# Two mixture-of-experts stages of a perceiver kernel: the order of norms, logits and first-layer products, who splits the weights, and the order of the output products

## The reference, cut to what matters

```python
xn = layernorm(x)                                    # (2048, 128), no gain or bias
logits = xn @ Wr + br                                # (2048, 8)
# mixture 1: probs = softmax(logits); comb = probs where in the token's top 2, else 0
y1 = sum(comb[:, e] * (gelu(xn @ W1[e] + b1[e]) @ W2[e] + b2[e]) for e in range(8))    # hidden 192
# mixture 2: comb = softmax over the top 2 logits alone
y2 = sum(comb[:, e] * ((silu(xn @ W1[e] + b1[e]) * (xn @ W2[e] + b2[e])) @ W3[e] + b3[e])
         for e in range(8))                                                            # hidden 512
x = x + y
```

## Time and profile before

| what | value |
| --- | --- |
| median of three runs | 3657.43 us (3654.14 to 3657.65) |
| the profiled execution, its own time | 3659.62 us |
| its span in the trace | 3656.9 us |
| PE busy over the span | 3368.5 us (92%) |
| DVE, ACT, POOL busy | 2508.6, 1895.5, 1145.4 us |
| mixture 1, from its first transfer to the last copy on ACT | 1280.6 to 1427.7 us |
| mixture 2, from its first transfer to the last addition on DVE | 3264.1 to 3650.3 us |

### The profile page before, as it was taken

The page is one execution under the profiler, slowest core; times in us unless marked ns, Lnnn a source line. Parts: engine busy times, 40 slices in busy tenths (PEclk is TensorE's granted clock), DMA queues, the critical chain, the costliest instruction groups (busy, mean ns, idle before and its releaser), DMA issues. The chain is left out here.

```text
span 3656.9 us, 83216 instructions
## 1 busy us (share of the span) xinstructions
PE 3368.5 (92%) x32913; PEld 2372.4 (65%) x32913; DVE 2508.6 (69%) x7162; ACT 1895.5 (52%) x2944; POOL 1145.4 (31%) x807
## 2 busy tenths in 40 slices
PE   6879999999997787999999999999999998957998
PEld 4646666666665665777777777777777776634555
DVE  5657777778785444777777777777777776675333
ACT  4336666666664222666666666666666664522332
POOL 1043333333331003433444334443344431233000
PEclk9969999999999688999999999999999999978999
DMA  1023333333330011111111111111111101000000
GB/s 52 2 68 75 81 71 76 76 78 73 75 65 1 2 47 41 42 33 35 37 42 42 33 36 37 42 42 33 30 42 42 42 22 47 1 27 1 1 1 12
DMA packets 95125, 146.43 MB, mean 40 GB/s; under 512 B 14961, under 2 KB 72337, under 8 KB 93969
## 3 DMA queue, kind: packets, MB, share of 16 engines
q1 hardware_dynamic: 94736, 141.12, 14.4%
HBM read 100.66 MB, written 1.05 MB: 28 GB/s over the span
## 5 line engine op out<-in xcount | busy, mean ns | idle before, releaser
L2137 DVE SCALAR_TENSOR_TENSOR arena<-banks,arena 128x512 f16<-128x512 f32 (+1 forms) x1024 | 554.4, 583 | 309.2 <-ACT arena L2226 307.9
L2226 ACT ACTIVATE arena<-banks 128x512 f16<-128x512 f32 (+1 forms) x1024 | 471.4, 512 | 399.5 <-PE banks L2044 396.4
L1092 DVE TENSOR_REDUCE arena<-banks 128x1 f32<-128x512 f32 (+1 forms) x896 | 529.1, 627 | 187.1 <-PE banks L977 181.8
L1189 ACT ACTIVATE arena<-banks 128x1024 f32<-128x1024 f32 (+1 forms) x448 | 425.0, 964 | 315.1 <-PE banks L998 312.2
L2149 DVE CUSTOM_DVE_ANT_0 arena<-banks,arena 128x1024 f32<-128x1024 f32 (+1 forms) x512 | 494.3, 987 | 31.0 <-issue 30.7
L2233 ACT ACTIVATE arena<-arena 128x1601 f32<-128x1601 f32 x256 | 417.7, 1632 | 107.3 <-DVE arena L2155 105.3
L2044 PE MATMUL banks<-consts,arena 128*128 128x128 f32 (+1 forms) x3328 | 457.6, 276 | 7.4 <-DVE arena L2137 6.6
L2058 PE MATMUL banks<-arena 128*128 128x256 f16 (+1 forms) x1664 | 456.2, 274 | 0.7 <-ACT arena L2240 0.7
L2060 PE MATMUL banks<-arena 128*128 128x256 f16 (+1 forms) x1664 | 451.3, 271 | 0.0
L2059 PE MATMUL banks<-arena 128*128 128x256 f16 (+1 forms) x1664 | 450.2, 271 | 0.0
L2044 PEld LDWEIGHTS banks<-consts,arena 128*128 128x128 f32 (+1 forms) x3328 | 365.6, 141 | 17.6 <-issue 10.5
(11 more groups left out here) (364 smaller groups left out, 6144.6 us busy)
## 6 DMA issues: line engine op xcount, KB each, us to landing
arena<-in_ctxT SPq DMA_DIRECT2D x64, 800.5 KB, 4.5
arena<-arena SPq DMA_DIRECT2D x768, 50.0 KB, 2.2
arena<-in_ctx SPq DMA_DIRECT2D x32, 768.0 KB
arena<-in_mask SPq DMA_DIRECT2D x32, 200.1 KB, 4.5
arena<-in_m2w SPq DMA_DIRECT2D x3, 2048.0 KB, 8.4
arena<-in_xw SPq DMA_DIRECT2D x1, 2048.0 KB, 11.6
weights<-in_weights SPq DMA_DIRECT2D x1, 1920.0 KB, 7.7
arena<-in_ctx SPq DMA_DIRECT2D x32, 32.5 KB
```

The source lines that it names most:

```text
L1092: eng.tensor_reduce(o, s, AX, ALU.max).then_inc(a_max, 1)
L1189: eng.activation(pr[0:w, at % 4, :].rearrange("p (x n) -> p x n", x=2)[:, :, 0:n], c.ps[0:w, bank:bank + 2, 0:n], ACT.Exp, scale=scale).th ...
L2137: eng.scalar_tensor_tensor(out=part(ptl, g, gr), in0=turned(gr), scalar=TOP, in1=part(pth, g, gr), op0=ALU.mult, op1=ALU.subtract).then_in ...
L2226: eng.activation(part(pth, g, gr), turned(gr), ACT.Copy, scale=TOP).then_inc(t_high, 1)
```

## The change

In both mixtures the front goes group by group: statistics, POOL's power and normalising with `Norms`, then transposes, logits and one unit on PE before the next group's transposes. In mixture 2, PE waits before a group's first unit for that group's split of x alone. The weights of an expert are split by ACT (`split_high`: scale and round, two instructions of 128x512) and DVE (`split_low`: scale again and take the rest, two more); POOL does none of it. The output products of mixture 2 are cut in two halves of two tiles, with two hidden units ahead of each half; the slots for hidden units go from 4 to 8 there. The steps to the combination stand between DVE's products of units 3 to 7. In mixture 1 the biases follow the third expert instead of the second, and ACT copies the turned queries out 12 units later. Transposes use PSUM banks 7 and 5 in turn.

```diff
 def pe(eng):                                   # both layers
-        for g in range(GROUPS): (transposes of all tiles into banks 0 to 3)
-        for g in range(GROUPS): (logits of all tiles)
...
+        turn(0)
+        logits(0)
+        hidden(0)
+        turn(1)
+        hidden(1)
+        logits(1)
+        turn(2)
+        hidden(2)
+        logits(2)
+        turn(3)
+        if two:
+            hidden(3)
+        logits(3)
...
+        else:
+            for r in range(GROUPS * E):
+                for half in range(2):
+                    n = FT * (r + 1) + 2 * half
+                    if n < last:
+                        hidden(n)
+                        hidden(n + 1)
+                    results(r, range(2 * half, 2 * half + 2))
+                if r % E == BIAS:
+                    biases(r // E)
...
-                if n == 0:
-                    eng.wait_ge(t["x_high"], GROUPS)
-                    eng.wait_ge(t["x_low"], GROUPS)
-                if g == 0 and u % FT == 0:
-                    eng.wait_ge(t["split"], e + 1)
+            if u == 0:
+                eng.wait_ge(t["x_low"], g + 1)
+            if g == 0 and u % FT == 0:
+                eng.wait_ge(t["w_low"], 2 * e + 2)
...
     def act(eng):
+        def split_high(e):
+            if e == 0:
+                eng.wait_ge(t["factor"], 1)
+            for x in range(2):
+                eng.activation(wh[:, x, e, :], w12.raw[:, x, e, :], ACT.Identity, scale=factor[:, x, e:e + 1]).then_inc(t["w_high"], 1)
...
+        copy_x(0)
+        if two:
+            split_high(0)
+        hidden(0)
+        if two:
+            split_high(1)
+        copy_x(1)
+        hidden(1)
+        copy_x(2)
+        hidden(2)
+        copy_x(3)
+        if two:
+            hidden(3)
+        exps()
...
+                if n >= 2 * units and n % units == units - 1:
+                    turn_queries(n // units - 2)
...
+                if n % FT == 0 and n // FT + 1 < E:
+                    split_high(n // FT + 1)
     def pool(eng):
...
-            for e in range(E):
-                w = w12.raw[:, :, e, :]
-                eng.tensor_tensor(w, w, spread(per_peak[:, :, e], F2), ALU.mult).then_inc(t["scaled"], 1)
-                eng.wait_ge(t["scaled"], e + 1)
-                eng.tensor_tensor(wh[:, :, e, :], w, one, ALU.mult).then_inc(t["high"], 1)
-                eng.wait_ge(t["high"], e + 1)
-                eng.tensor_tensor(wl[:, :, e, :], w, wh[:, :, e, :], ALU.subtract).then_inc(t["split"], 1)
     def dve(eng):
+        def split_low(e):
+            if e == 0:
+                eng.wait_ge(t["factor"], 1)
+            for x in range(2):
+                eng.wait_ge(t["w_high"], 2 * e + x + 1)
+                eng.scalar_tensor_tensor(out=wl[:, x, e, :], in0=w12.raw[:, x, e, :], scalar=factor[:, x, e:e + 1],
+                                         in1=wh[:, x, e, :], op0=ALU.mult, op1=ALU.subtract).then_inc(t["w_low"], 1)
...
+        measure(0)
+        if two:
+            peaks()
+        measure(1)
+        normed(0)
+        if two:
+            factors()
+        measure(2)
...
+            low_x(0)
+            split_low(0)
+            second_biases()
+            normed(1)
+            measure(3)
+            product(0)
+            normed(2)
+            low_x(1)
+            product(1)
+            split_low(1)
+            normed(3)
+            low_x(2)
+            product(2)
...
+            low_x(3)
+            product(3)
+            shifted_logits()
+            product(4)
+            best()
+            product(5)
+            split_low(2)
+            mark()
+            product(6)
+            combine()
+            product(7)
+            results(0)
+            for n in range(2 * FT, last):
+                product(n)
+                if n % FT == 1 and n // FT + 1 < E:
+                    split_low(n // FT + 1)
+                if n % FT == FT - 1:
+                    results(n // FT - 1)
```

More of the change, by code:

```diff
@@ L1557, in mixture @@
     N = PAIRS
-    if layer == 1:
+    one_layer, two = layer == 1, layer == 2
+    if one_layer:
         w1, w3 = k.f32(E * F1), k.f32(2 * E * D)
-        units, bias, router, row = U1, "m1_b1", "r1", "br1"
+        units, bias, router, row, NH, BIAS = U1, "m1_b1", "r1", "br1", 4, 2
         need = lambda e: [(3 * e // 2, 2 * e), (3 * e // 2 + 1, 2 * e + 1)]
+        xw = k.f32(4, HP * D)
+        q_norms = Norms(c, k, "q1")
+        q = {n: c.sem(f"q1_{n}") for n in ("w_loaded", "fold_psum", "folded", "turned_psum", "xT")}
     else:
@@ L1581, in mixture @@
     comb, combT = k.f32(N, E), k.f32(P)
-    NH = 4
     hT = k.f32(NH, G * P)
[L1584 to L1587, removed]
+    gate = k.f32(2, G * P) if two else None
+    names = ["w_loaded", "sentinels", "turned_psum", "xT", "logits", "biased", "max", "shifted", "exps", "sums", "recips", "probs",
+             "top8", "marked", "chosen", "comb", "combT_psum", "combT", "bias_psum", "bias_added", "hidden_psum", "gate", "hidden",
+             "out_psum", "out_added"]
     s = {n: c.sem(f"{nm}_{n}") for n in names}
[L1589 to L1592, removed]
     A = c.A
@@ L1653, in results @@
+        def results(r, js):
+            g, e = r // E, r % E
+            if js[0] == 0:
+                wait_if(eng, s["out_added"], r - 1)
+                eng.wait_ge(s["hidden"], g * units + need(e)[-1][0] + 1)
+            if r == 0:
+                eng.wait_ge(t["peak_spread"], 1) if two else None
+            if r == 1:
+                eng.wait_ge(s["xT"], GROUPS)
+                if two:
+                    eng.wait_ge(t["x_low"], GROUPS)
+            for j in js:
                 for x, (u, wo) in enumerate(need(e)):
@@ L1670, in fold @@
         def fold(f):
-            a, t = f // 4, f % 4
+            a, tt = f // 4, f % 4
             if f == 0:
@@ L1737, in turn_queries, with hidden @@
             eng.activation(xT(g), c.ps[:, 2 + g % 2, :], ACT.Copy).then_inc(q["xT"], 1)
-        folds = {(need(e)[-1][0] + 3): e for e in range(E)}
-        for n in range(GROUPS * units):
+        def hidden(n):
             u = n % units
[L1742 to L1747, removed]
             eng.wait_ge(s["hidden_psum"], n + 1)
-            if layer == 1:
+            if one_layer:
                 free_hidden(eng, n)
@@ L1912, in mixture @@
+    if two:
+        assert k.at <= w12.low
     m.engines = dict(sp=sp, pe=pe, dve=dve, act=act, pool=pool)
-    if layer == 2:
-        assert k.at <= w12.low
-    m.after = [(s["out_added"], GROUPS * E), (s["bias_added"], GROUPS)] + ([(q["xT"], GROUPS)] if layer == 1 else [])
+    m.after = [(s["out_added"], GROUPS * E), (s["bias_added"], GROUPS)] + ([(q["xT"], GROUPS)] if one_layer else [])
     return m
```

344 lines of the change are left out of this document (178 added, 166 removed).

## The result

The changed kernel takes 3565.52 us (median of 4 runs, 3562.10 to 3577.74), the kernel before beside it 3656.61 (4 runs): ratio 0.9762, interval 0.9742 to 0.9781 (the two medians alone give 0.9751). Predicted were 3575.0, range 3566 to 3597: the median lies 9.5 us under the forecast, right at the lower end of the range (0.5 us under the rounded 3566). The profiled execution took 3577.74 us, the longest of its four; a second one was taken later (experiment e9).

| us | start to mixture 1 | mixture 1 | between | mixture 2, to the store's issue | after it | span |
| --- | --- | --- | --- | --- | --- | --- |
| before | 1280.6 | 148.3 | 1835.2 | 386.2 | 6.6 | 3656.9 |
| after, first | 1276.5 | 142.3 | 1844.7 | 305.9 | 6.6 | 3576.0 |
| after, second (e9) | 1269.6 | 137.9 | 1843.0 | 305.8 | 6.6 | 3562.9 |

The account below looks back on a forecast made before the run. PE waits bound the kernel: mixture 2's front on DVE held by POOL, its rounds on unit latency. Savings of 39.7 + 36.9 + 4.5 + 2.4 = 83.5 us gave 3575 us, own range 3566 to 3589, eight-in-ten range 3566 to 3597.

Parts of the forecast that it names:

- Rounds: Mixture 2 after the tenth unit: halves between units remove PE's waits, 8.82 us a round, 39.7 us saved.
- the 1.16 us: Late round of mixture 2: 9.98 us less 8.82 of PE's work, read as two waits on a unit's latency.
- (b): Mixture 2's rounds: products or additions come out of PE's order, 1.16 us stay in 31 rounds, 3611 us; chance 0.10.
- Front of mixture 2: Unit 0 starts at 9.1 us instead of 44.1, unit 9 ends at 37.7 instead of 74.6: 36.9 us saved.
- Table load: Mixture 2's front: three loads instead of one, 1.28 us each, one on the path; the skill's drain not charged.
- POOL beside DVE: Mixture 2's front: by the skill's exclusion rule, POOL's small power steps would delay normalising, 0.5 us on the path.
- Mixture 1: Front 4.5 us shorter, with three results done at 31.5 us, plus 2.4 us from the turned queries' later place.
- The turned queries: Mixture 1: their later copy on ACT ends a Gelu's wait at three experts, 2.4 us saved.
- (a): Mixture 2's front: DVE's list runs late, unit 9 ends at 50 us and splits hold PE, 3591 us; chance 0.12.
- (c): PE stays at 1.2 GHz after mixture 2's front, 8.8 us more a round, 3681 us with 12 such rounds; chance 0.02.
- (d): Mixture 1 gains nothing because the combination's chain ends later, 3582 us; counted inside the forecast's 0.76.

Follow-up runs that it names:

- e9: The changed kernel run once more, on one chip with the kernel before and the e8 version: 3564.90 us, ratio 0.9767.
- e1: The changed kernel with whole runs of output products in mixture 2 (four units, then 32 passes) instead of halves: ratio 0.9808 to the kernel before.
- e5: The kernel before with only mixture 2's halves, eight slots and additions behind an expert's last product: ratio 0.9894.
- e2: The changed kernel with the weights' split given back to POOL, order by groups kept: ratio 0.9831 to the kernel before.
- e3: The kernel before with only the weights' split of mixture 2 moved from POOL to ACT and DVE: ratio 0.9938.
- e4: The kernel before with only mixture 1 in its new form, mixture 2 as before: ratio 0.9989 over 10 runs.
- e8: The changed kernel with later combination steps and splits, later waits for output weights, and x stored in four group transfers: 3557.21 us, ratio 0.9744.

## Why the prediction was right, point by point

- **Rounds** (39.7 us): right in mechanism, slightly low. From the tenth unit to the end of PE's work are 3568.1 - 3299.2 = 268.9 us, against 310.4 before: 41.5. I had 8.82 us a round; measured is 8.75, since half a run takes 1.79 us (3482.55 to 3484.34) and not 1.83; times 31 that is the 2 us. No gap stands at a switch. But my reading of the 1.16 us was wrong in two ways, and the forecast was lucky in the first. I counted 24 products between 3635.37 and 3645.35; that is the kernel's last round, with 18, and its waits are 2.45 us. The full rounds ahead happen to take 9.98 us too, so the 1.16 stand. And they aren't two waits of one latency but three (e1): 0.52 is the latency, 0.38 the place of the additions, which I had only under rival (b), as a danger, and 0.22 that PE worked only one unit ahead. The change closes all three, so the sum held.
- **Front of mixture 2** (36.9 us): right. Unit 0 at 8.9 us (9.1), tenth unit at 35.7 (37.7), saved 38.9. The four waits are 0.68, 0.42, 1.01 and 0.78 us where I had 1.0, 0.9, 1.5 and 1.0. The splits, which had no row, cost 0.66 and 0.70 us each (0.6 and 0.7 taken).
- **The parts add up.** Halves, with the slots and the later additions that belong to them, give 40.8 us alone (e5). The groupwise front with the combination's steps between products, added to them, gives 16.8 (from e5's 345.4 to e2's 328.7), and the split on top 22.8 (to 305.9). The split alone, in the old order, gives 22.6 (e3): nearly the same sum from other waits, DVE's slow normalising in e3, and in e2 also the first split and PE's clock.
- **Table load.** 3286.57 + 1.28 is 3287.85, and ACT's next instruction starts at 3287.86. The drain of 1.38 us of the Trainium skill (ScalarE: Activation LUTs, What ACT_TABLE_LOAD costs) shows in no row here; the row was the better price.
- **POOL beside DVE.** The power step at 3266.93 lies beside normalising at 3266.49, whose four instructions take 1.07 us; the 16 of the front, most of them beside no power step, range from 303 to 348 ns. The rule of the Trainium skill (SBUF — State Buffer, SBUF: two separate sides) isn't borne out for POOL's 128x4 instruction, and e2 bears it out for the long ones of 128x1024: 5.80 us for four.
- **Mixture 1** (6.9 us): the sum was right for the first execution (6.0), for a partly wrong reason. The combination ends at 26.9 us (26.6 said). Three results are done at 33.5, and not at 31.5, and I had the wrong thing last: the third was to wait for the first addition, to 27.8, but it starts at 30.0 with no wait in its row. PE's own work came last, part of it at a clock that I had taken for full (0.59 from 1296.81 to 1301.00): the first run of output products takes 3.05 us and the products for the next stage behind it 1.23, where e9, at 0.98 and more from 11.4 us on, has 2.03 and 0.72. In e9 the stage gained 10.4. The turned queries gave 2.8 (2.4).
- **Rivals.** (a) is refuted: unit 9 is not late, and no split of weights holds a unit. (b) is refuted: no row of PE in a late round names a wait. (c) is refuted: 1.00 from 3301 on. (d) is refuted by e4's 139.1 us.
- **What I had not priced:** unchanged code. It moved by 4 us one way and 9.4 the other, more than mixture 1's whole gain. 3575 was 9.5 above the median: the mixtures gave 3 us more than said in the first execution and 7 in e9, and the rest is such code, as far as the profiled executions tell; the other three executions of that kernel have no trace.

## What to carry to other kernels

When PE waits for the engine behind it by a fixed latency, put independent products of at least that length between a unit and its successor in the same banks, and look first at which instruction of the waited-for engine stands ahead of the needed one: of the 1.1 us that a round lost here, 0.5 was latency and 0.6 was order and how far PE worked ahead. POOL instructions of two microseconds beside short DVE instructions can stretch each of those from 0.34 us to 2. In a kernel with sparse stages compare stage by stage, since the same code moved by 3 us in 20 and by 8 in 180 here, with the granted clock.

## What the runs showed of the hardware beyond that

One program, two executions: mixture 1 takes 142.3 and 137.9 us with the same instructions. The stage before mixture 2 takes 175.7 to 177.5 us in eight of the twelve profiles and 181.0 to 185.4 in four; between 120 and 130 us after the stage's first transfer the slow ones have a clock of 0.50 to 0.68, the others at least 0.84, and both executions of one program fell on the same side each time (185.4 and 184.2; 176.2 and 177.5 for e8).

Not every DVE instruction waits for POOL. In e2, beside POOL's long instructions, normalising takes up to 1.93 us instead of 0.34, a copy from `arena` to `arena` (128x128) 1.23 instead of 0.23 and a subtraction there 2.11 instead of 0.29. The products of units, which read a PSUM bank, keep 0.73 to 0.75 us, and 15 searches for the best eight keep their 1.20 us in all.
